# One static order of 512-query chunks through a two-attention transformer block

## The reference

```
xn1 = LN(x)                                 # g1, be1
x   = x + causal_attention(xn1, xn1) @ W1 + b1
xn2 = LN(x)                                 # g2, be2
x   = x + attention(xn2, ctx) @ W2 + b2
xn3 = LN(x)                                 # g3, be3
out = x + relu(xn3 @ Wf1 + bf1) @ Wf2 + bf2   # 1024 hidden channels
attention: scores = q k^T * 4, softmax, times v   # "scores / scale", scale = 16 ** -0.5
```

## Time and profile before

| | us |
|---|---|
| median of the runs (3) | 627.12 (626.6 to 629.98) |
| span of the profiled execution | 631.5 |
| TensorE busy | 504.7 (80%) |
| VectorE busy | 368.2 (58%) |
| ScalarE busy | 307.5 (49%) |
| GpSimd busy | 187.8 (30%) |
| DMA queue of SyncE, share of 16 engines | 38.1% |

### The profile page before, as it was taken

The page is one execution under the profiler, slowest core; times in us unless marked ns, Lnnn a source line. Parts: engine busy times, 40 slices in busy tenths (PEclk is TensorE's granted clock), DMA queues, the critical chain, the costliest instruction groups (busy, mean ns, idle before and its releaser), DMA issues.

```text
span 631.5 us, 8807 instructions
## 1 busy us (share of the span) xinstructions
PE 504.7 (80%) x3296; PEld 296.2 (47%) x3296; DVE 368.2 (58%) x695; ACT 307.5 (49%) x590; POOL 187.8 (30%) x276
## 2 busy tenths in 40 slices
PE   1775775999997999799988835669576757989887
PEld 0664452344443444344333333434222446988877
DVE  4887697678886788678532147645221763454430
ACT  3544020667765776477666502247443535253460
POOL 3788821131221132122132523305131350121200
PEclk9988697799999999899999969767555968999998
DMA  8138936007367335727260266978333212101001
GB/s 288 47 109 158 201 116 118 0 21 116 52 120 105 67 66 107 115 56 38 83 186 1 68 168 92 173 108 140 107 99 115 81 47 72 34 0 34 18 17 34
DMA packets 41930, 56.51 MB, mean 89 GB/s; under 512 B 12832, under 2 KB 27424, under 8 KB 41888
## 3 DMA queue, kind: packets, MB, share of 16 engines
q1 hardware_dynamic: 39584, 47.56, 38.1%
q10 hardware_dynamic: 2304, 8.39, 3.8%
HBM read 35.12 MB, written 20.42 MB: 88 GB/s over the span
## 4 chain that ended last, share of the span: by engine, by line
PE 44%; DMA 23%; DVE 15%; ACT 6%; SPq 5%; issue 3%; POOL 2%; ACTq 0%; DVEq 0%
PE ps L864 10%; PE ps L973 9%; PE ps L948 8%; PE ps L911 7%; DMA arena_h<-heads 6%; DMA stacks<-shift_t 6%; PE ps L1060 5%; DMA recips<-recip_rows 4%; DVE max_a L1141 4%; ACT arena_p L732 4%; DMA heads<-out_t 4%; DVE xn L1094 3%; SPq L409 2%; PE ps L933 2%; SPq L428 2%
## 5 line engine op out<-in xcount | busy, mean ns | idle before, releaser
L732 ACT ACTIVATE arena_p<-ps 128x512 f32<-128x512 f32 (+4 forms) x416 | 190.9, 541 | 129.5 <-PE ps L948 127.3
L1141 DVE TENSOR_REDUCE max_a<-ps 128x1 f32<-128x512 f32 (+4 forms) x280 | 159.6, 620 | 46.6 <-PE ps L911 34.0
L948 PE MATMUL ps<-stacks 99*128 99x512 bf16 (+2 forms) x448 | 149.9, 369 | 27.6 <-DMA stacks<-shift_t 22.5
L911 PE MATMUL ps<-stacks 96*128 96x77 bf16 (+4 forms) x640 | 146.2, 306 | 32.1 <-DVE max_a L1141 19.1
L911 PEld LDWEIGHTS ps<-stacks 96*128 96x128 bf16 x640 | 58.9, 111 | 97.5 <-DVE max_a L1141 45.5
L973 PE MATMUL ps<-arena_p,v_group 128*32 128x512 f32 (+4 forms) x896 | 94.1, 540 | 0.7 <-POOL arena_p L617 0.5
L617 POOL TENSOR_SCALAR_AFFINE_SELECT arena_p<-arena_p 128x512 f32<-128x512 f32 x64 | 41.0, 653 | 169.9 <-ACT arena_p L732 169.9
L948 PEld LDWEIGHTS ps<-stacks 99*128 99x128 bf16 (+1 forms) x448 | 45.6, 107 | 93.1 <-ACT arena_p L732 37.8
L1141 DVE TENSOR_REDUCE max_b<-ps 128x1 f32<-128x384 f32 (+3 forms) x88 | 52.5, 636 | 21.3 <-PE ps L915 21.3
L864 PE MATMUL ps<-wf2r,hid_r 128*128 128x256 f32 x384 | 49.9, 294 | 9.6 <-DVE hid_r L1254 9.6
L864 PEld LDWEIGHTS ps<-wf2r,hid_r 128*128 128x128 f32 x384 | 49.1, 202 | 10.7 <-DVE hid_r L1254 10.7
(11 more groups left out here) (68 smaller groups left out, 528.1 us busy)
## 6 DMA issues: line engine op xcount, KB each, us to landing
heads<-out_t ACTq DMA_DIRECT2D x16, 512.0 KB, 4.3
stacks<-q_parts SPq DMA_DIRECT2D x48, 128.0 KB, 5.2
stacks<-k_parts SPq DMA_DIRECT2D x48, 128.0 KB, 7.6
stacks<-qc_parts SPq DMA_DIRECT2D x48, 128.0 KB, 5.1
arena_h<-heads SPq DMA_DIRECT2D x8, 512.0 KB
recips<-recip_rows SPq DMA_DIRECT2D x8, 512.0 KB
q_parts<-parts SPq DMA_DIRECT2D x8, 384.0 KB, 2.5
k_parts<-parts SPq DMA_DIRECT2D x8, 384.0 KB, 2.6
```

The source lines that it names most:

```text
L732: nc.scalar.activation(probs[0:a.kp, a.probs_slot(g, ui), h, k * BANK:k * BANK + width], ps[0:a.kp, unit % S_BANKS, 0:width], ACT.Exp, sca ...
L911: ins = nc.tensor.matmul(m_bank(use)[:, o:o + w], q_stack[0:ROWS, g % a.nb, h, t * P:(t + 1) * P], k_rows(ROWS, g, h, s0, s0 + w), start=T ...
L948: ins = nc.tensor.matmul(ps[0:keys, unit % S_BANKS, lo - k * BANK:hi - k * BANK], k_rows(ROWS_S, g, h, i * P, i * P + keys), q_stack[:, g ...
L1141: nc.vector.tensor_reduce(dst, m_bank(use)[:, 0:nh * w].rearrange("p (h w) -> p h w", h=nh), AX.X, ALU.max).then_inc(s.max_read, 1)
```

## The change

The unit of work becomes a `Job`: four heads of one chunk of 512 queries, 16 for the causal attention (eight over 512 keys, "half 0", eight over 1024 keys, "half 1") and 16 for the cross attention. A `Plan` gives every piece of work of the whole kernel a key and sorts them into one list. TensorE, VectorE, ScalarE, GpSimd and SyncE each walk this list and do their part of each item. A causal job of half 0 spans 10 keys, one of half 1 spans 26, so the causal scores lie at keys 0 to 288. The rest of the work is put between them by keys written out by hand.

```diff
+    S_RING, M_RING, X_RING, O_RING = [0, 1, 2], [3, 4, 5], [6], [7]
+        for j in self.self_jobs:
+            j.cost = 26 if j.half else 10
+            groups = [[4], [5, 7], [6], [0], [1], [2], [3]] if self.half else [[0], [1, 3], [2]]
+    def divide(self, kind, n, pair, at):
+        self.add(at, "heads", kind, n, pair)
+        self.add(at + 3.0, "recip", kind, n, pair)
+        self.add(at + 6.0, "spread", kind, n, pair)
+        self.add(at + 9.5, "div", kind, n, pair)
+        def ahead(m):
+            return m - 22 - 14 * min(1, m / 60)
...
+                self.add(ahead(s[x] + j.cost * done / sum(weights)), "chunk", j, c)
+            self.add(ahead(s[x + 1]) + 3, "shift", j)
+            self.wanted.append((ahead(s[x]) - 12 if x >= GB else (-63.9, -63.8, -57, -56.9)[x], j))
...
+                    self.add(s[x] + j.cost * (done + w * h / GH) / sum(widths), "score", j, st, h)
...
+        self.norm(0, 0, -80, bias=5)
+        self.norm(0, 1, -73, gap=11, bias=12)
+        self.norm(0, 2, 24)
+        self.norm(0, 3, 68)
+        self.project(0, -68, 3, 1)
+        self.project(1, -30, 4, 2)
+        self.project(2, 36, 4.5, 2.5)
+        self.project(3, 80, 4.5, 2.5)
...
+        for n in range(NCH):
+            done = s[4 * n + 4] + 4
+            tail = n == NCH - 1
+            self.divide("self", n, 0, s[4 * n + 2] + 9)
+            self.divide("self", n, 1, done + 3)
+            at = done + 14
+            for half in range(2):
+                self.add(at + half, "w1", n, half)
+            self.norm(1, n, at + 2.5, low=False, gap=3.2)
+            for hh in range(2):
+                self.unit(at + 10 + 3.5 * hh, ("qc", n, hh))
+            base, span = (at + 28, 5) if tail else (at + 30, 9)
+            for gg in range(GB):
+                cross(self.cross_jobs[GB * n + gg], base + span * gg, span)
...
+            at = base + 3 * span + 34
+            for half in range(2):
+                self.add(at + half, "w2", n, half)
+            start = (end + 2, end + 36, end + 70, at + 12)[n]
+            step = 4.2 if n < 3 else 2.6
...
+            for f in range(NF):
+                self.add(start + step * f, "hid", n, f)
+                self.add(start + step * f + 1.4, "hidlow", n, f)
+                self.add(start + step * (f + 2) - 0.3, "ffo", n, f)
```

The parts go to DRAM six-fold, in the order in which the stack wants them, with the channels of four heads reordered on the host. A block of a stack (512 columns) is then loaded by one DMA, the shift rows by one DMA, and six K and seven Q blocks are reused:

```diff
+                for first, n, part in ((0, 3, 0), (3, 2, 1), (5, 1, 2)):
+                    src = parts[:, slot, part:part + 1, :].to_broadcast([P, n, CHUNK]) if queries \
+                        else parts[:, slot, 0:n, :]
+                    sp.dma_start(dram[first:first + n].rearrange("p g r t -> (g r) p t"), src)\
+                        .then_inc(parts_out[slot], 16)
...
+                sp.dma_start(stacks[0:ROWS, b, :, :].rearrange("p h t -> p (h t)"),
+                             src.rearrange("s (d h) t -> s d (h t)", h=GH)).then_inc(block_in[b], 16)
...
+                sp.dma_start(stacks[ROWS:ROWS_S, qb, :, :].rearrange("k h (i t) -> k (h i) t", t=P), shift_t[:, p, :])\
+                    .then_inc(shift_in[qb - K_BLOCKS], 16)
```

```diff
+                nc.vector.scalar_tensor_tensor(out=rest[:, x % 2, 0:width], in0=bank_of(("proj", u))[:, 0:width],
+                                               scalar=col[:, c:c + 1], in1=parts[:, x % PART_SLOTS, 0, 0:width],
+                                               op0=ALU.add, op1=ALU.subtract).then_inc(frees(("proj", u)), 1)
...
+                pool.tensor_copy(p[:, 1, :], rest[:, x % 2, 0:width]).then_inc(part_b, 1)
+                pool.wait_ge(part_b, x + 1)
+                pool.tensor_tensor(p[:, 2, :], rest[:, x % 2, 0:width], p[:, 1, :], ALU.subtract).then_inc(part_c, 1)
...
+                pool.wait_ge(recip_in[x % 2], 16 * (x // 2 + 1))
+                o = heads[:, heads_of(kind == "self", n), pair, :]
+                pool.tensor_tensor(o, o, recips[:, x % 2, :], ALU.mult).then_inc(heads_done, 1)
...
+                        ins = nc.tensor.matmul(o[32 * h:32 * h + VW, q0:CHUNK], value_rows(j, i, h),
+                                               probs[0:j.kp, slot, h, off:off + w], start=(st == 0 and x == 0),
+                                               stop=last, skip_group_check=True)
```

More of the change, by code:

```diff
@@ L90, in __init__ @@
         self.chunks = []
[L91 to L94, removed]
+        for t in range(CT):
+            keys_t = self.half * CHUNK + (t + 1) * P if causal else S_CTX
+            for s0 in range(0, keys_t, BANK):
+                w = min(BANK, keys_t - s0)
                 nh = min(BANK // w, GH)
-                self.chunks += [(t, h, nh, s, w) for h in range(0, GH, nh)]
@@ L98, in __init__ @@
[L98 to L114, removed]
-                at += c
-            return out
-        unit_at = spread([self.unit_width(u) + BANK for u in range(len(self.units))])
-        chunk_at = spread([nh * w + 64 for _, _, nh, _, w in self.chunks])
-        stream = [(g + chunk_at[c], ("chunk", g, c)) for g in range(NG) for c in range(len(self.chunks))]
-        stream += [(g + 1 + gap, ("shift", g)) for g in range(NG)]
-        for n, (first, second, normed) in enumerate(rows):
-            stream += [(first + lead, ("rows", n, 0)), (second + lead, ("rows", n, 1)), (normed + lead, ("norm", n))]
-        stream.sort(key=lambda e: e[0])
-        self.pe, self.uses = [], []
-        def use(what):
-            if what[0] == "norm":
-                self.pe.append(what)
-                return
-            self.pe.append(("m", len(self.uses)))
-            self.uses.append(what)
-        for g in range(NG):
-            for u, (ui, h, k) in enumerate(self.units):
-                while stream and stream[0][0] <= g + unit_at[u] + lead:
-                    use(stream.pop(0)[1])
-                self.pe.append(("score", g, u))
-                if u + 1 == len(self.units) or self.units[u + 1][0] != ui:
-                    if ui:
-                        self.pe.append(("product", g, ui - 1))
-                    elif g:
-                        self.pe.append(("product", g - 1, self.n_steps - 1))
-        for _, what in stream:
-            use(what)
-        self.pe.append(("product", NG - 1, self.n_steps - 1))
-        self.use_at = {what: i for i, what in enumerate(self.uses)}
@@ L170, in masks @@
-    def masks(self, g, ui):
-        return self.kt * g + sum(len(pieces) for pieces, _ in self.steps[:ui + 1])
-    def probs_slot(self, g, ui):
-        return (self.n_steps * g + ui + (not self.causal)) % P_SLOTS
-SELF = Attention(True, T, buffers=3, lead=1.35, gap=0.12, rows=[(6.8, 6.9, 7.15), (7.3, 7.4, 7.6)])
-CROSS = Attention(False, S_CTX, buffers=5, lead=2.3, gap=0.5, rows=[(7.05, 7.15, 7.55), (7.6, 7.7, 7.99)])
-SELF_EARLY = [14, 18, 22, 26, 30, 36, 44]
-CROSS_EARLY = [12, 16]
+                self.chunks += [(t, h, nh, s0, w) for h in range(0, GH, nh)]
```

1821 lines of the change are left out of this document (937 added, 884 removed).

## The result

| | before | after | forecast |
|---|---|---|---|
| median of the runs, us | 627.12 | 704.26 (701.28 to 704.61, 3 runs) | 564 |
| span of the profiled execution | 631.5 | 702.5 | 568 |
| first causal score | 111.6 | 85.4 | 75 |
| first to last causal score | | 417 | 344 |
| from the last causal score to the end | | 200 | 149 |

The changed kernel is slower: 1.1208 times the time of before, 95% interval 1.1117 to 1.13. The forecast was 564 us, with 634 as the upper end of its range.

What follows compares the result with a forecast made beforehand. TensorE was taken to bound the kernel. Prologue 75, causal stretch 344 and tail 149 us sum to 568 us of span, less 4.4 for the runs' median, so 564 us; 525 to 634 was given about 8 in 10.

Steps and rivals of the forecast that it cites:

- What bounds the kernel now: Whole kernel: TensorE, busy 504.7 of 631.5 us; its idle 127 us are the most a better order alone can win.
- The work that was woven in: Causal stretch: middle of chunks 0 to 2, 72 us, and projections, 25, beside 240 causal, minus 8: 329 us.
- I take 15 us for all (bounds 0 and 100): Causal stretch: stops at shifts, block loads, divisions and the product's single bank, 15 us, making 344 us.
- The clock, left at 0.97: Causal stretch: without pauses TensorE's granted clock should be the earlier causal stage's 0.97, against 0.83 and 0.68 in the middle.
- Tail, 149 us: After the last causal score: chunk 3's middle 24, feed-forward 100, last addition and store 5, waits 20 (10 to 45).
- Prologue, 75 us: Before the first causal score: first chunks at about 48 us, first score at 75 (65 to 88), 37 us earlier.
- Rival 2: Half-1 jobs' first chunk and score: loads come too late, 72 us of waits, span 640, time 636; chance 18%.
- The mark I set for it: Sign of Rival 2: TensorE's waits on the stacks' loads or shifts over 40 us in total.
- Rival 3: Divisions, mostly on GpSimd: stops at their upper end, 10 us more in the tail, 593 us span; chance 17%.
- Rival 4: Products with 17 columns: four heads don't run side by side, 48.9 us become 196, over 710 us; chance 2%.
- 88 us of the middle: Middle of chunks 0 to 2: three quarters of 118 us of TensorE work, 63 fully scaled by clock, 72 taken.
- rival 1: Whole kernel: TensorE never starves, 68 + 320 + 129 = 517 us of span, 513 of time; chance 10%.

Runs made afterwards that it cites:

- e8: e5 with the whole division left out, its three transfers too: 621.8 us, ratio 0.992 to the kernel before.
- e5: Changed kernel with block loads of 96 outermost rows and the heads' stores issued from ScalarE's queue: 668.5 us, ratio 1.067 to the kernel before.
- e6: e5 with VectorE's remainder of the hidden chunk later in the list: 657.9 us, ratio 1.052 to the kernel before.
- e1: Changed kernel with parts stored so that a block load has 96 outermost rows for six, a unit's store being six DMAs: 681.6 us, ratio 1.083.
- e2: Changed kernel with three parts stored by one DMA a unit and each block loaded by six DMAs of 16 rows: 684.8 us, ratio 1.091.
- e4: Changed kernel with the memset of the stacks' extra rows moved behind the eighth unit's parts: 701.8 us, ratio 1.118.
- e15_nodiv2: e6 with longer leads of the second and last norm and e4's later memset, without the division and its transfers: 619.7 us, ratio 0.988.
- e3: Changed kernel with the heads' stores issued from ScalarE's queue, so SyncE's list no longer waits for the product's copy: 691.6 us, ratio 1.100.
- e11: e6 with the shift as three DMAs, as before the change: 672.5 us, ratio 1.069.
- e7: e5 with longer leads for the division's inverse, spreading and multiplication, and W1 and W2 products 4 keys later: 669.0 us, ratio 1.068.
- e9: e5 without VectorE's inverse, SyncE storing the sums as they came: 658.0 us, ratio 1.044.
- e10: e5 without GpSimd's multiplication, the W products still waiting for the spread sums: 659.7 us, ratio 1.048.

## Why the prediction was wrong

The sum missed the span by 134 us: prologue 10, causal stretch 73, tail 51.

1. *What bounds the kernel now, and the work itself: right.* The 329 us of TensorE work for the causal stretch were measured as 341 at a clock of 0.92 and as 320 at 0.99. The work that was woven in is as cheap as forecast.
2. *"I take 15 us for all (bounds 0 and 100)": this step failed.* The stops were 417 - 341 = 76 us, so 61 of the 73 us (and 355 - 320 = 35 even in e8). The durations were priced well: one block load took 6.38 us, the upper end of the forecast 2 to 6.3, three together 12.3 for 6 to 19. What failed is the wait: I had priced a late transfer by what TensorE alone would wait for it. With one list for all, a late item holds its engine, the items behind it are late on other engines, and the next transfer is issued late in turn. That is read from the chain, where single late transfers stop VectorE and TensorE together; what the runs measure are the shares, out of 704: load shape 23, the heads' store off SyncE's list and queue 13, division 47 (of which 27 are its transfers and SyncE's waits, which I had not priced: I had VectorE and GpSimd waiting, not SyncE). The division reaches into the tail as well.
3. *The clock, left at 0.97.* The granted clock is 0.92 in the causal stretch and 0.84 in the tail. It rose whenever stops were taken out (e5 0.95 in 80 to 470, e8 0.99 in 80 to 435). The pauses cost twice: as such, and some 21 us (341 against 320) as slower matmuls, for busy time times clock is about the same in both (314 and 317). That the clock's fall comes from the pauses is what the order of these runs suggests; no run changed one without the other.
4. *Tail, 149 us: too low by 51.* The 24 + 100 us of work became 152 at a clock of 0.84, 28 us more. Most of it is the clock: e8_nodiv has 143 at 0.90, and busy time times clock is 128 and 129, which is an estimate of this work at full clock; the stops were 201 - 152 = 49 us instead of 25. The forecast took each feed-forward chunk at its pace of before, where TensorE met nobody in a list; the ring of waits (e6: 10.5 us) is new.
5. *Prologue, 75 us: 10 low, inside its bounds.* The first chunk came at 46.3 us for 48, so the 10 us lie behind it: 39 us from there to the first score for the 27 of the forecast. With the faster block loads the first score comes at 81 (e1, e2, e5); that is 5 of the 10. What the memset costs stays open (e4).
6. *The rivals.* Rival 2 had the right side, at 18%, and half its mechanism: the shape of the loads and the place of the heads' store cost 36 us (e5), not 72, and what came late behind the loads were stores and loads of heads, not shifts. The mark I set for it, over 40 us of TensorE's waits on loads and shifts, was a bad one: they are 23 us while the cure gave 36. Rival 3, the divisions, had 25 us and was 47, and SyncE's part was missing. I priced the two as alternatives, and they came together, with the tail's ring and the clock on top. Rival 4 did not occur: the wide product takes 664 ns, beside its neighbours.
7. *Two slips in the working, without weight.* By the clocks of the earlier trace rows, 88 us of the middle scale to 65 and not 63 us. And rival 1's 513 us lies below 525, so all of its 10% is below the range, not "little of" it; the 8 in 10 already leave it out.

Of the load rule of the Trainium skill ("DMA: Bandwidth & Descriptors", section "Why a DMA increments its semaphore by 16 and not by 1", the number of engines is the largest up to 16 that divides the slowest dimension): 96 outermost rows for six took 22.7 us off the kernel (e1), and six loads of 16 outermost rows took 19.5 us off it (e2). The direction agrees; the count of engines is not in any row here.

What stays open: with all cures, e15_nodiv2 has no division and is still 1% faster than before only, against 10% forecast. In its profiled execution, which is 7 us shorter than its median, the causal part is 356 us against the 344 forecast, and the tail 175 against 149. I haven't taken the tail's 26 us apart further. Nor was the causal stage given a larger lead for the heads' chains by another order of jobs.

## What to carry to other kernels

When several engines walk one list, price a late item by everything behind it on its engine, and follow it once round the other engines and the DMA queue, SyncE's list included; a price per item, added up, was too low here by five times (15 us against 76). Alternatives that can occur together are not rivals: give their sum a chance of its own. Before relying on prefetch leads, look at the outermost dimension of each load and at what is issued right behind it, stores and loads alike.

## What the runs showed that I had not expected

- How unevenly one kind of transfer lands: the same 256 KB store took 2.1 us in the median of 32 and 9.6 at worst, and the long ones stood behind a burst of parts stores and block loads. From ScalarE's queue it still took up to 6.8 us (e3), while SyncE's own queue did no worse than 4.1 once the loads went out as small DMAs (e2).
- The price of added DMAs depends on where they stand: 64 more for the shifts cost 14.6 us by the medians and 11 by the ratios (e11), 160 more for parts and blocks 3 us (e2 against e1).
- Taking 34 us of VectorE's waits away (e7) changed the time by nothing, while leaving out one engine's share of the division (e9, e10) gave 9 to 15 us each: the total of a wait row says little of what it is worth.
